# An expert layer in one block: gate and up products made while VectorE routes, eight of them multiplied on GpSimd

## The chip, the cores and the metric

The kernel runs on one NeuronCore of a Trainium2 chip. The metric is the device time of one execution in microseconds. TensorE (PE) multiplies matrices into eight PSUM banks of 128x512 f32; VectorE (DVE) and ScalarE (ACT) read and write PSUM and SBUF; GpSimd (POOL) works on SBUF only; SyncE (SP) issues transfers.

## The reference, cut to what matters

A decoder of four layers over 1024 tokens of 128 features. Every sublayer's output is added to x and normalised. The sublayer in question is the expert layer of the third layer, L2_ffn: a mixture of 8 experts of 176 hidden units, with the two best experts of each token.

```
probs = softmax(x @ router_w.T); topk_w, topk_idx = top_k(probs, 2)
topk_w = topk_w / (sum(topk_w) + 1e-20)
combine = sum(topk_w[..., None] * one_hot(topk_idx, E), axis=1)
for e in range(E):
    g = x @ w_gate[e].T;  u = x @ w_up[e].T
    ye = silu(g) * u @ w_down[e].T
    out = out + combine[:, e:e + 1] * ye
```

## The kernel before

x is kept in SBUF as 128 features by 1024 tokens. The 8 x 176 hidden units lie side by side as M = 11 groups of 128; with two halves of 512 tokens that makes 22 items (m, h), and every token goes through every expert, weighted with `combine`, which is zero for those not chosen. A stage is a row of blocks; all engines leave a block before any begins the next, and the semaphores are cleared between. L2_ffn has four blocks before its norm.

- Router, by the helper `stream` (L136): eight f32 matmuls of x against the router's 8 columns into one bank (recorded at L163), and VectorE copies the 64 logits to `probs` (L1901). SyncE starts the next stage's weights.
- Route (L1903 to L1953): VectorE makes the softmax (Exp on ScalarE, L1911), the eight largest (L1925) and their places (L1928), the shares of the first two, `combine` (L1941), and splits it into three bf16 parts in `parts` (L1944 to L1947). GpSimd clears `parts` (L1951), casts the 0/1 matrix `spread` to bf16 (L1952) and centres w_down by the helper `weight_centring` (L217, L221, L222). TensorE has nothing in this block.
- Turn (L1954): eight bf16 matmuls turn `parts`, and VectorE copies two banks to `partsT` (L1957).
- Experts (L1958 to L2008): `centre_tokens` (L230) starts the sums in banks 6 and 7. Then for item j three matmuls (L1975): gate, up, and spread against `partsT`, which gives the item's weight for each token. They go into banks 0 to 2 or 3 to 5 by j's parity. ScalarE takes the silu of gate (L1997), VectorE multiplies with up (L2007) and with spread (L2008) into `hidden`, and TensorE adds w_down's product to bank 6 or 7 (L1982). TensorE's order is up(0), up(1), down(0), up(2), down(1), ...; up(j) waits until item j-2 is multiplied, down(j) until item j is.

The norm that follows reads banks 6 and 7. Engines run their instructions in order.

Of the kernel before, what the change touches and what calls it, by code (L numbers as in the profile page):

```python
# [20 lines left out]
ACT = mybir.ActivationFunctionType  # L21
ALU = mybir.AluOpType
# [179 lines left out]
def weight_centring(K, stack, tag, groups, scratch=None):  # L202

    nc = K.nc
    if scratch is None:
        scratch = stack.enter_context(nc.sbuf_tensor(f"{tag}_weight_sums", [P, groups, P // 2], F32))
    sem = Sems(nc, stack, tag + "_centre")
    own, ready = sem("pool_own"), sem("weights_centred")  # L210

    def centre(pool, w):
        chain = Chain(pool, own)
        w, half = w.rearrange("p (g c) -> p g c", c=P), P // 2
        src = w
        while half >= 1:
            chain.link(nc.gpsimd.tensor_tensor(scratch[:, :, 0:half], src[:, :, 0:half], src[:, :, half:2 * half],  # L217
                                               ALU.add))
            src, half = scratch, half // 2
        mean = scratch[:, :, 0:1]  # L220
        chain.link(nc.gpsimd.tensor_scalar(mean, mean, 1 / P, None, ALU.mult))  # L221
        nc.gpsimd.tensor_tensor(w, w, mean.to_broadcast([P, groups, P]), ALU.subtract).then_inc(ready, 1)  # L222
    return centre, ready
# [757 lines left out]
def halves(ap):  # L981
    return [ap[:, h * HALF:(h + 1) * HALF] for h in range(2)]
# [896 lines left out]
def L2_ffn(K):  # L1879
# [7 lines left out]
    with ExitStack() as stack:  # L1887
        def sb(name, shape, dt=F32):
# [6 lines left out]
        parts, rest = sb("parts", [P, 2 * B, 3, 32], BF16), sb("rest", [P, 2 * B, E])  # L1895
        partsT, spread = sb("partsT", [96, T], BF16), sb("spread", [96, M * P], BF16)
        silu, hidden = sb("silu", [P, 2, HALF]), sb("hidden", [P, 2, HALF])
        centre_w_down, _ = weight_centring(K, stack, "L2_ffn", M)
        stream(K, "L2_ffn_router", [
            ("dve", P, [(c * E, E, [(x[:, c * P:(c + 1) * P], W("router"))]) for c in range(2 * B)],  # L1900
             lambda bank: nc.vector.tensor_copy(probs[:].rearrange("p c e -> p (c e)"), bank[:, 0:2 * B * E]))],  # L1901
            on_sync=K.fetch_next)
        with ExitStack() as inner:  # L1903
            sem = Sems(nc, inner, "L2_ffn_route")
            own, shifted, exp_done, cleared = sem("dve_own"), sem("shifted"), sem("exp_done"), sem("cleared")
            block = inner.enter_context(nc.Block())

            @block.scalar
            def _(act):
                act.wait_ge(shifted, 1)  # L1910
                nc.scalar.activation(probs[:], probs[:], ACT.Exp).then_inc(exp_done, 1)  # L1911

            @block.vector
            def _(dve):
                chain = Chain(dve, own)
                wide = lambda ap: ap.to_broadcast([P, 2 * B, E])
                chain.link(nc.vector.tensor_reduce(stat[:], probs[:], AX.X, ALU.max))
                nc.vector.tensor_tensor(probs[:], probs[:], wide(stat[:].unsqueeze(2)), ALU.subtract
                                        ).then_inc(shifted, 1)
                dve.wait_ge(exp_done, 1)  # L1920
                chain.link(nc.vector.tensor_reduce(stat[:], probs[:], AX.X, ALU.add))
                chain.link(nc.vector.reciprocal(stat[:], stat[:]))
# [21 lines left out]
                chain.link(nc.vector.tensor_copy(part[0], combine[:]))  # L1944
                chain.link(nc.vector.tensor_tensor(rest[:], combine[:], part[0], ALU.subtract))
                chain.link(nc.vector.tensor_copy(part[1], rest[:]))
                nc.vector.tensor_tensor(part[2], rest[:], part[1], ALU.subtract)  # L1947

            @block.gpsimd
            def _(pool):  # L1950
                nc.gpsimd.memset(parts[:], 0.0).then_inc(cleared, 1)  # L1951
                nc.gpsimd.tensor_copy(spread[:], W("spread"))  # L1952
                centre_w_down(pool, W("w_down"))  # L1953
        stream(K, "L2_ffn_turn", [  # L1954
            ("dve", 96, [(c * P, P, [(parts[:, 4 * c4 + c].rearrange("p r e -> p (r e)"), K.ident_bf)])
                         for c in range(4)],
             lambda bank, c4=c4: nc.vector.tensor_copy(halves(partsT)[c4], bank[0:96, :])) for c4 in range(2)])  # L1957
        with ExitStack() as inner:  # L1958
            sem = Sems(nc, inner, "L2_ffn_experts")
            up_done, silu_done, own, hidden_done, down_done = (sem(n) for n in (  # L1960
                "up_done", "silu_done", "dve_own", "hidden_done", "down_done"))
            block = inner.enter_context(nc.Block())

            items = [(m, h) for m in range(M) for h in range(2)]

            @block.tensor
            def _(pe):
                def up(j):
                    m, h = items[j]
                    if j >= 2:  # L1970

                        pe.wait_ge(hidden_done, j - 1)
                    for n, (w, rhs) in enumerate(((W("w_gate"), halves(x)[h]), (W("w_up"), halves(x)[h]),
                                                  (spread, halves(partsT)[h]))):
                        last = nc.tensor.matmul(K.bank[3 * (j % 2) + n][:], w[:, m * P:(m + 1) * P], rhs,  # L1975
                                                start=True, stop=True)
                    last.then_inc(up_done, 1)

                def down(j):
                    m, h = items[j]  # L1980
                    pe.wait_ge(hidden_done, j + 1)
                    nc.tensor.matmul(K.bank[6 + h][:], W("w_down")[:, m * P:(m + 1) * P], hidden[:, j % 2], start=False, stop=(m == M - 1),  # L1982
                                     skip_group_check=True).then_inc(down_done, 1)
                centre_tokens(K, K.bank[6:8])
                for j in range(len(items) + 1):
                    if j < len(items):
                        up(j)
                    if j >= 1:
                        down(j - 1)

            @block.scalar
            def _(act):
                for j in range(len(items)):
                    act.wait_ge(up_done, j + 1)
                    if j >= 2:
                        act.wait_ge(hidden_done, j - 1)
                    nc.scalar.activation(silu[:, j % 2], K.bank[3 * (j % 2)][:], ACT.Silu).then_inc(silu_done, 1)  # L1997

            @block.vector
            def _(dve):  # L2000
                chain = Chain(dve, own)
                for j in range(len(items)):
                    dve.wait_ge(silu_done, j + 1)
                    if j >= 2:
                        dve.wait_ge(down_done, j - 1)
                    hj = hidden[:, j % 2]
                    chain.link(nc.vector.tensor_tensor(hj, silu[:, j % 2], K.bank[3 * (j % 2) + 1][:], ALU.mult))  # L2007
                    nc.vector.tensor_tensor(hj, hj, K.bank[3 * (j % 2) + 2][:], ALU.mult).then_inc(hidden_done, 1)  # L2008
        norm_of_centred(K, "L2_ffn_norm", K.bank[6:8])


# [646 lines left out]
```

## Time and profile before

| | |
|---|---|
| time, median of 3 | 1590.61 us (1590.35 to 1593.66) |
| profiled execution, its own time | 1582.52 us |
| its span, first to last instruction | 1580.7 us |
| TensorE busy | 1209.8 us, 77% |
| VectorE / ScalarE / GpSimd busy | 984.1 / 881.5 / 543.8 us |
| granted TensorE clock, mean | 0.892 |

The profile is one execution. Each row has a start from the span's begin and a duration; matmuls overlap in their pipeline, so their durations sum to more than the time. The granted clock is 1.00 at 2.4 GHz and 0.50 at 1.2 GHz. L2_ffn lies between 951 and 1035 us.

### The profile page before, as it was taken

Reading aid. Unit: us, or ns where it says so; the run is one execution under the profiler, and the core shown is the slowest. Engines: PE = TensorE matmul, PEld = TensorE weight load, DVE = VectorE, ACT = ScalarE, POOL = GpSimd, SP = SyncE. Lnnn points to the kernel's source line nnn. Section 1 sums busy time; section 2 is a strip of 40 time slices with the busy share of each in tenths; the row PEclk is TensorE's granted clock in tenths of the full one; section 3 lists DMA queues with packets and bytes.
Section 4 is the critical chain, followed back from the end, with each engine's and each line's share of the span. In section 5 each row is a group of like instructions: output and inputs, shape, how many; then the busy total and the mean of one; then the engine's idle time right before and its main releaser. Section 6 shows DMA issues by size and latency. Waiting matters only on the chain. (4 is left out here: it accounts for less than half of the span.)

```text
span 1580.7 us, 21176 instructions
## 1 busy us (share of the span) xinstructions
PE 1209.8 (77%) x6990; PEld 607.2 (38%) x6990; DVE 984.1 (62%) x1994; ACT 881.5 (56%) x1817; POOL 543.8 (34%) x673
## 2 busy tenths in 40 slices
PE   8999647266666677987657995977968988979886
PEld 3675422022222233542213552433444434734562
DVE  3673455999999927632757735446546658727752
ACT  3674144599999926874124871234634745724643
POOL 1462014488888843200224212011101223503440
PEclk9999887599999987998877997987986999999998
DMA  3000000000000015101006200015114110000000
GB/s 149 2 2 1 22 9 0 0 0 0 1 0 0 0 73 141 22 34 40 0 3 196 50 2 18 0 33 124 16 56 125 37 56 1 2 1 1 1 2 13
DMA packets 44108, 48.75 MB, mean 31 GB/s; under 512 B 3808, under 2 KB 40800, under 8 KB 42848
## 3 DMA queue, kind: packets, MB, share of 16 engines
q1 hardware_dynamic: 40688, 45.83, 10.0%
q10 hardware_dynamic: 3312, 1.57, 0.3%
q8 instruction: 56, 0.92, 0.3%
q14 instruction: 52, 0.43, 0.1%
HBM read 34.28 MB, written 13.11 MB: 30 GB/s over the span
## 5 line engine op out<-in xcount | busy, mean ns | idle before, releaser
L1548 POOL TENSOR_TENSOR L_attn_z<-L_attn_state,L_attn_r 128x1024 f32<-128x1024 f32 x64 | 151.0, 2360 | 21.6 <-DVE L_attn_state L1534 14.7
L1534 DVE TENSOR_TENSOR_SCAN L_attn_state<-bank,L_attn_w 128x512 f32<-128x512 f32 x128 | 148.9, 1205 | 0.0
L1445 PE MATMUL bank<-L_attn_z,const 128*128 128x512 f32 x256 | 139.4, 673 | 0.2 <-POOL L_attn_z L1552 0.2
L950 DVE CUSTOM_DVE_ANT_0 L_xattn_core_logits<-bank,L_xattn_mask 128x256 f32<-128x256 f32 x256 | 98.6, 422 | 45.1 <-PE bank L722 32.6
L1429 PE MATMUL bank<-L_attn_rows,L_attn_select 128*128 128x512 bf16 x96 | 36.2, 435 | 79.5 <-ACT L_attn_C L1497 42.9
L1485 ACT ACTIVATE L_attn_r<-L_attn_after_dt,L_attn_half_guard,L_attn_A 128x512 f32<-128x512 f32 x128 | 96.5, 802 | 0.0
L1475 ACT ACTIVATE bank<-L_attn_dt,L_attn_A 128x510 f32<-128x510 f32 x128 | 86.5, 676 | 12.8 <-DVE L_attn_state L1534 12.8
L862 ACT ACTIVATE L_xattn_core_probs<-bank 128x512 f32<-128x512 f32 x132 | 71.6, 596 | 35.6 <-PE bank L765 24.5
L1552 POOL TENSOR_TENSOR L_attn_z<-L_attn_z,L_attn_C 128x1024 f32<-128x1024 f32 x32 | 75.8, 2368 | 23.4 <-ACT L_attn_C L1497 23.3
L1515 DVE TENSOR_TENSOR L_attn_w<-bank,L_attn_udt 128x1024 f32<-128x1024 f32 x64 | 78.2, 1221 | 5.3 <-PE bank L1429 1.6
L722 PE MATMUL bank<-L_xattn_core_rows 48*128 48x256 bf16 x384 | 61.3, 302 | 17.2 <-DVE L_xattn_core_top L950 11.9
L1445 PEld LDWEIGHTS bank<-L_attn_z,const 128*128 128x128 f32 x256 | 54.3, 212 | 49.2 <-issue 39.8
L543 POOL TENSOR_TENSOR L_attn_core_probs<-L_attn_core_probs,L_attn_core_rsum 128x256 f32<-128x256 f32 x64 | 51.6, 827 | 60.5 <-DVE L_attn_core_rsum L512 60.5
L543 POOL TENSOR_TENSOR L_ffn_core_probs<-L_ffn_core_probs,L_ffn_core_rsum 128x256 f32<-128x256 f32 x64 | 51.6, 829 | 45.9 <-DVE L_ffn_core_rsum L512 45.9
L2313 PE MATMUL bank<-L_ffn_shifted,weights 128*128 128x512 f32 x128 | 61.1, 622 | 8.0 <-PEq L2232 8.0
L217 POOL TENSOR_TENSOR L_attn_weight_sums<-weights 128x64 f32<-128x64 f32 (+1 forms) x3 | 1.1, 365 | 191.0 <-POOLq L306 110.8
L1491 ACT ACTIVATE L_attn_r<-L_attn_r 128x1024 f32<-128x1024 f32 x64 | 66.7, 1043 | 0.0
L163 PE MATMUL bank<-x,weights 128*128 128x512 f32 (+1 forms) x108 | 52.9, 639 | 12.8 <-PEq L306 5.8
L2399 POOL TENSOR_TENSOR L_ffn_part<-L_ffn_part 128x512 f32<-128x512 f32 x32 | 40.8, 1274 | 61.4 <-DVE L_ffn_part L2378 61.4
L920 POOL TENSOR_TENSOR shiftsT<-L_xattn_core_top,nothing 128x8 bf16<-128x8 f32 x48 | 12.1, 253 | 142.3 <-DVE L_xattn_core_top L950 95.6
L477 ACT ACTIVATE L_ffn_core_probs<-bank,L_ffn_core_negmax 128x128 f32<-128x128 f32 (+1 forms) x128 | 52.0, 428 | 9.6 <-DVE L_ffn_core_negmax L503 9.6
L750 PE MATMUL bank<-L_xattn_core_rows 48*128 48x256 bf16 x384 | 56.7, 283 | 0.4
(500 smaller groups left out, 3042.9 us busy)
## 6 DMA issues: line engine op xcount, KB each, us to landing
L_xattn_core_rows<-L_xattn_core_slots SPq DMA_DIRECT2D x48, 96.0 KB, 2.3
L_xattn_core_rows<-L_xattn_core_slots SPq DMA_DIRECT2D x12, 384.0 KB, 6.1
weights<-in_pack_L_ffn SPq DMA_DIRECT2D x2, 2118.5 KB, 8.1
L_xattn_core_slots<-L_xattn_core_k_parts SPq DMA_DIRECT2D x24, 128.0 KB, 2.1
weights<-in_pack_L_ffn SPq DMA_DIRECT2D x1, 2824.0 KB, 12.3
L_xattn_core_slots<-L_xattn_core_q_parts SPq DMA_DIRECT2D x9, 192.0 KB, 2.2
weights<-in_pack_L_xattn SPq DMA_DIRECT2D x1, 1539.5 KB, 6.3
weights<-in_pack_L_attn SPq DMA_DIRECT2D x2, 768.0 KB, 9.4
```

What stands on the lines that cost most here:

```text
L543: last = nc.gpsimd.tensor_tensor(part, part, rsum[:, i % NB, :, sc:sc + 1].to_broadcast([P, 2, keys[sc].stop]), ALU.mult)
L722: last = nc.tensor.matmul(scores_bank[side][:, c * S:(c + 1) * S], row(QUERIES, side, p, c), row(KEYS, side, p), start=True, stop=True)
L862: nc.scalar.activation(probs[n % 3][:, at], shifted_bank[at][:], ACT.Exp).then_inc(exp_done, 1)
L950: last = nc.vector.tensor_tensor_reduce(logits[:, c], scores_bank[side][:, c * S:(c + 1) * S], mask[:, 2 * b + c, :], 1.0, MASKED, ALU.add ...
L1445: last = nc.tensor.matmul(y_bank[2 * c + half][:], ident, z[:, g % NS, c], start=False, stop=False, skip_group_check=True)
L1475: nc.scalar.activation(two(a_bank[c][:])[:, :, lo:lo + S - 1], two(dt[d][:, c, tokens(half)])[:, :, lo:lo + S - 1], ACT.Exp, scale=A[d][:, ...
L1485: last = nc.scalar.activation(r[:, g % NS, c], after_dt[d][:, c, tokens(half)], ACT.Tanh, bias=half_guard[:], scale=A[d][:, 1, at:at + 1])
L1491: nc.scalar.activation(r[:, g % NS], r[:, g % NS], ACT.Copy, scale=0.5, bias=0.5).then_inc(r_done, 1)
L1515: nc.vector.tensor_tensor(w[:, g % 2], B_bank[:].unsqueeze(1).to_broadcast([P, DC, HALF]), udt[d][:, :, tokens(half)], ALU.mult).then_inc( ...
L1534: nc.vector.tensor_tensor_scan(state[:, g % NS, c, ::step], a_bank[c][:, ::step], w[:, g % 2, c, ::step], 0.0, ALU.mult, ALU.add).then_inc ...
L1548: nc.gpsimd.tensor_tensor(z[:, g % NS], state[:, g % NS], r[:, g % NS], ALU.mult).then_inc(z_done, 1)
L1552: nc.gpsimd.tensor_tensor(z[:, g % NS], z[:, g % NS], copied[:, g // 2 % 2].unsqueeze(1).to_broadcast([P, DC, HALF]), ALU.mult).then_inc(p ...
```

## The change

The four blocks become one. TensorE does the router into bank 2, the centring matmuls, then gate and up (without spread) of items 0 to 9. For items 0 to 7 (EARLY = 8) ScalarE empties both banks, silu of gate and a copy of up, into a new SBUF tile `ahead` (32 KB a partition), and GpSimd multiplies the two after it has centred w_down. Items 8 and 9 stay in the banks. up(j) waits for the copies of item j-2, as far as there are any. Then TensorE waits for `parts`, turns them through banks 2 and 5, waits for `spread`, `partsT` and the centred w_down, and goes through the items: up(j) from j = 10 on, spread as a step of its own, `weigh(j)`, which waits until item j-2 is multiplied, and down(j-1). VectorE multiplies an early item once (`ahead` by the spread bank) and the other 14 twice, as before. ScalarE waits for gate and up, no longer for spread.

```diff
-        centre_w_down, _ = weight_centring(K, stack, "L2_ffn", M)
-        stream(K, "L2_ffn_router", [
-            ("dve", P, [(c * E, E, [(x[:, c * P:(c + 1) * P], W("router"))]) for c in range(2 * B)],
-             lambda bank: nc.vector.tensor_copy(probs[:].rearrange("p c e -> p (c e)"), bank[:, 0:2 * B * E]))],
-            on_sync=K.fetch_next)
+        centre_w_down, w_down_ready = weight_centring(K, stack, "L2_ffn", M)
+        EARLY = 8
+        ahead = sb("ahead", [P, EARLY, 2, HALF])
...
+            spread_bank = K.bank[2:6:3]
...
+            @block.sync
+            def _(sp):
+                K.fetch_next(sp)
+
+            @block.tensor
+            def _(pe):
+                def up(j):
+                    m, h = items[j]
+                    if 2 <= j < EARLY + 2:
+                        pe.wait_ge(taken_ahead, 2 * min(EARLY, j - 1))
+                    elif j >= 2:
+                        pe.wait_ge(hidden_done, j - 1)
+                    for n, w in enumerate((W("w_gate"), W("w_up"))):
+                        last = nc.tensor.matmul(K.bank[3 * (j % 2) + n][:], w[:, m * P:(m + 1) * P], halves(x)[h],
+                                                start=True, stop=True)
+                    last.then_inc(up_done, 1)
+
+                def weigh(j):
+                    m, h = items[j]
+                    if j >= 2:
+                        pe.wait_ge(hidden_done, j - 1)
+                    nc.tensor.matmul(spread_bank[j % 2][:], spread[:, m * P:(m + 1) * P], halves(partsT)[h],
+                                     start=True, stop=True).then_inc(spread_done, 1)
...
+                for c in range(2 * B):
+                    last = nc.tensor.matmul(spread_bank[0][:, c * E:(c + 1) * E], x[:, c * P:(c + 1) * P], W("router"),
+                                            start=True, stop=True)
+                last.then_inc(router_done, 1)
+                centre_tokens(K, K.bank[6:8])
+                for j in range(EARLY + 2):
+                    up(j)
+                pe.wait_ge(parts_ready, 1)
+                for c4 in range(2):
+                    for c in range(4):
+                        last = nc.tensor.matmul(spread_bank[c4][0:96, c * P:(c + 1) * P],
+                                                parts[:, 4 * c4 + c].rearrange("p r e -> p (r e)"), K.ident_bf,
+                                                start=True, stop=True)
+                    last.then_inc(turned, 1)
+                pe.wait_ge(spread_ready, 1)
+                pe.wait_ge(partsT_ready, 2)
+                pe.wait_ge(w_down_ready, 1)
+                for j in range(len(items) + 1):
+                    if j < len(items):
+                        if j >= EARLY + 2:
+                            up(j)
+                        weigh(j)
+                    if j >= 1:
+                        down(j - 1)
 
             @block.scalar
             def _(act):
                 act.wait_ge(shifted, 1)
                 nc.scalar.activation(probs[:], probs[:], ACT.Exp).then_inc(exp_done, 1)
+                for j in range(EARLY):
+                    act.wait_ge(up_done, j + 1)
+                    nc.scalar.activation(ahead[:, j, 0], K.bank[3 * (j % 2)][:], ACT.Silu).then_inc(taken_ahead, 1)
+                    nc.scalar.activation(ahead[:, j, 1], K.bank[3 * (j % 2) + 1][:], ACT.Copy).then_inc(taken_ahead, 1)
+                for j in range(EARLY, len(items)):
+                    act.wait_ge(up_done, j + 1)
+                    if j >= EARLY + 2:
+                        act.wait_ge(hidden_done, j - 1)
+                    nc.scalar.activation(silu[:, j % 2], K.bank[3 * (j % 2)][:], ACT.Silu).then_inc(silu_done, 1)
...
+                nc.vector.tensor_tensor(part[2], rest[:], part[1], ALU.subtract).then_inc(parts_ready, 1)
+                for c4 in range(2):
+                    dve.wait_ge(turned, c4 + 1)
+                    nc.vector.tensor_copy(halves(partsT)[c4], spread_bank[c4][0:96, :]).then_inc(partsT_ready, 1)
+                for j in range(len(items)):
+                    hj = hidden[:, j % 2]
+                    if j >= 2:
+                        dve.wait_ge(down_done, j - 1)
+                    if j < EARLY:
+                        dve.wait_ge(product_ahead, j + 1)
+                        product = ahead[:, j, 0]
+                    else:
+                        dve.wait_ge(silu_done, j - EARLY + 1)
+                        chain.link(nc.vector.tensor_tensor(hj, silu[:, j % 2], K.bank[3 * (j % 2) + 1][:], ALU.mult))
+                        product = hj
+                    dve.wait_ge(spread_done, j + 1)
+                    nc.vector.tensor_tensor(hj, product, spread_bank[j % 2][:], ALU.mult).then_inc(hidden_done, 1)
 
             @block.gpsimd
             def _(pool):
                 nc.gpsimd.memset(parts[:], 0.0).then_inc(cleared, 1)
-                nc.gpsimd.tensor_copy(spread[:], W("spread"))
+                nc.gpsimd.tensor_copy(spread[:], W("spread")).then_inc(spread_ready, 1)
                 centre_w_down(pool, W("w_down"))
...
+                for j in range(EARLY):
+                    pool.wait_ge(taken_ahead, 2 * (j + 1))
+                    nc.gpsimd.tensor_tensor(ahead[:, j, 0], ahead[:, j, 0], ahead[:, j, 1], ALU.mult).then_inc(product_ahead, 1)
```

The blocks of the turn and of the experts as they were are removed; `down(j)` is as it was.

## Rows read from the trace of the kernel before

**Rows 1.** Table of stretches (us; busy us and instructions by engine; granted clock; DMA).

```profile
951.10:953.20 2.10, 1.92 (x16) 1.86 (x16) 0.04 (x1) 0.00 (x0) 0.00 (x0) 1.00 0.46 112
953.20:956.00 2.80, 0.00 (x0) 0.00 (x0) 2.05 (x6) 0.26 (x1) 2.17 (x3) 0.57 0.38 155
956.00:965.30 9.30, 0.00 (x0) 0.00 (x0) 8.63 (x39) 0.00 (x0) 6.97 (x9) 0.50 0.00 1
...
971.00:1032.20 61.20, 61.01 (x153) 26.51 (x151) 29.00 (x43) 13.14 (x22) 0.00 (x0) 1.00 0.00 0
...
1034.70:1036.80 2.10, 0.00 (x0) 0.00 (x0) 0.00 (x0) 1.87 (x3) 0.00 (x0) 0.69 0.00 0
```

**Rows 2.** Timeline, TensorE, the router (start, duration, engine, line, operation, idle).

```profile
951.20 1.92 PE L163 MATMUL bank<-weights,x 128*128 128x8 f32 x16 [2.85 <-PEq L239]
```

**Rows 3.** Timeline, VectorE and GpSimd during the route.

```profile
953.83 0.74 POOL L1951 MEMSET L_ffn_parts<- 128x768 bf16 x1 [27.49 <-PEq L1903]
953.97 0.23 DVE L1918 TENSOR_TENSOR L_ffn_probs<-L_ffn_probs,L_ffn_stat 128x64 f32<-128x64 f32 x1
...
954.52 1.35 POOL L1952 CAST L_ffn_spread<-weights 96x1408 bf16<-96x1408 f32 x1
...
955.01 2.57 DVE L1923 TENSOR_TENSOR L_ffn_probs<-L_ffn_probs,L_ffn_stat 128x64 f32<-128x64 f32 x1
955.84 1.66 POOL L217 TENSOR_TENSOR L_ffn_weight_sums<-weights 128x704 f32<-128x704 f32 x1
...
961.05 2.56 POOL L222 TENSOR_TENSOR weights<-weights,L_ffn_weight_sums 128x1408 f32<-128x1408 f32 x1
...
964.96 0.23 DVE L1947 TENSOR_TENSOR L_ffn_parts<-L_ffn_rest,L_ffn_parts 128x64 bf16<-128x64 f32 x1
```

**Rows 4.** Timeline, from the turn to the first item of the loop.

```profile
965.45 0.88 PEld L163 LDWEIGHTS bank<-ident_bf,L_ffn_parts 128*96 128x96 bf16 x8 [12.42 <-issue]
...
966.15 1.28 DVE L1957 CAST L_ffn_partsT<-bank 96x512 bf16<-96x512 f32 x2 [0.97 <-PE bank L163]
967.72 1.28 ACT L1997 ACT_TABLE_LOAD   x1 [13.24 <-PEq L146]
...
967.76 3.39 PE L230 MATMUL bank<-x,const 128*128 128x512 f32 x4 [1.22 <-PEq L146]
...
970.98 1.88 PE L1975 MATMUL bank<-x,weights 128*128 128x512 f32 x4
...
975.22 1.13 PE L1982 MATMUL bank<-L_ffn_hidden,weights 128*128 128x512 f32 x2 [0.20 <-DVE L_ffn_hidden L2008]
```

**Rows 5.** Timeline, the loop: the fourth item, then the last.

```profile
978.97 1.88 PE L1975 MATMUL bank<-x,weights 128*128 128x512 f32 x4
...
1028.62 0.60 ACT L1997 ACTIVATE L_ffn_silu<-bank 128x512 f32<-128x512 f32 x1 [2.20 <-PE bank L1975]
...
1029.25 0.69 DVE L2007 TENSOR_TENSOR L_ffn_hidden<-L_ffn_silu,bank 128x512 f32<-128x512 f32 x1 [1.39 <-ACT L_ffn_silu L1997]
1029.29 1.88 PE L1975 MATMUL bank<-x,weights 128*128 128x512 f32 x4
...
1033.51 1.12 PE L1982 MATMUL bank<-L_ffn_hidden,weights 128*128 128x512 f32 x2 [1.27 <-DVE L_ffn_hidden L2008]
```

**Rows 6.** Groups by line and shape, GpSimd and ScalarE (count, busy, mean ns, idle).

```profile
L2399 POOL TENSOR_TENSOR L_ffn_part<-L_ffn_part 128x512 f32<-128x512 f32 x32 | 40.8, 1274 | 61.4 <-DVE L_ffn_part L2378 61.4
...
L868 ACT ACTIVATE L_xattn_core_gathered<-bank 128x512 f32<-128x512 f32 x4 | 2.4, 591 | 1.2 <-PE bank L781 1.2
```

**Rows 7.** Timeline, GpSimd and VectorE in an earlier stage.

```profile
270.83 2.17 POOL L1309 TENSOR_TENSOR L_attn_rows<-L_attn_left,L_attn_middle 32x1024 bf16<-32x1024 f32 x1
...
271.04 3.04 DVE L1348 SCALAR_TENSOR_TENSOR L_attn_dt<-L_attn_dt,L_attn_spare 128x1024 f32<-128x1024 f32 x1
```

**Rows 8.** Timeline, ScalarE in an earlier stage.

```profile
225.90 0.19 ACT L1276 ACTIVATE L_attn_half_guard<-const 128x1 f32<-128x1 f32 x1
...
227.36 1.06 ACT L1283 ACTIVATE L_attn_u<-L_attn_conv 128x1024 f32<-128x1024 f32 x1
```

More of the change, by code:

```diff
@@ new lines, in L2_ffn, with down @@
+        EARLY = 8
+        ahead = sb("ahead", [P, EARLY, 2, HALF])
+        items = [(m, h) for m in range(M) for h in range(2)]
+        with ExitStack() as inner:
+            sem = Sems(nc, inner, "L2_ffn_experts")
+            router_done, own, shifted, exp_done, cleared = (sem(n) for n in ("router_done", "dve_own", "shifted", "exp_done",
+                                                                            "cleared"))
+            spread_ready, parts_ready, turned, partsT_ready = (sem(n) for n in ("spread_ready", "parts_ready", "turned",
+                                                                                "partsT_ready"))
+            up_done, silu_done, taken_ahead, product_ahead = (sem(n) for n in ("up_done", "silu_done", "taken_ahead",
+                                                                               "product_ahead"))
+            spread_done, hidden_done, down_done = (sem(n) for n in ("spread_done", "hidden_done", "down_done"))
+            spread_bank = K.bank[2:6:3]
+            block = inner.enter_context(nc.Block())
+            @block.sync
[19 more added lines that the diff above has]
+                                     start=True, stop=True).then_inc(spread_done, 1)
+                def down(j):
+                    m, h = items[j]
+                    pe.wait_ge(hidden_done, j + 1)
+                    nc.tensor.matmul(K.bank[6 + h][:], W("w_down")[:, m * P:(m + 1) * P], hidden[:, j % 2], start=False,
+                                     stop=(m == M - 1), skip_group_check=True).then_inc(down_done, 1)
+                for c in range(2 * B):
[22 more added lines that the diff above has]
+                        down(j - 1)
@@ L1916, in _ @@
                 wide = lambda ap: ap.to_broadcast([P, 2 * B, E])
+                dve.wait_ge(router_done, 1)
+                chain.link(nc.vector.tensor_copy(probs[:].rearrange("p c e -> p (c e)"), spread_bank[0][:, 0:2 * B * E]))
                 chain.link(nc.vector.tensor_reduce(stat[:], probs[:], AX.X, ALU.max))
-                nc.vector.tensor_tensor(probs[:], probs[:], wide(stat[:].unsqueeze(2)), ALU.subtract
-                                        ).then_inc(shifted, 1)
+                nc.vector.tensor_tensor(probs[:], probs[:], wide(stat[:].unsqueeze(2)), ALU.subtract).then_inc(shifted, 1)
                 dve.wait_ge(exp_done, 1)
@@ L1951, in _ @@
                 nc.gpsimd.memset(parts[:], 0.0).then_inc(cleared, 1)
-                nc.gpsimd.tensor_copy(spread[:], W("spread"))
+                nc.gpsimd.tensor_copy(spread[:], W("spread")).then_inc(spread_ready, 1)
                 centre_w_down(pool, W("w_down"))
[L1954 to L2008, printed above, removed]
```

3 lines of the change are left out of this document (removed).

## The prediction

> **What bounds the kernel now.** I read the page first: TensorE is the busiest engine, but none bounds the whole, so the stage decides. The change touches only the expert layer, and the table of stretches cuts that layer into parts [rows 1]. From 951.1 to 953.2 TensorE does 16 tiny router matmuls; from 953.2 to 965.3 it does nothing while VectorE is busy 10.7 of 12.1 us (2.05 + 8.63, routing) and GpSimd 9.1; then come 2.5 us of turning the parts and, from 967.7, the centring matmuls [rows 4]; and from 971.0 to 1032.2 TensorE is busy 61.0 of 61.2 us. So the layer is a route during which TensorE waits, then a loop that TensorE alone bounds.
>
> The timeline gives the durations. A 512-column f32 matmul is two records; gate, up and down of an item are six, and the bf16 spread one that streams half as long. The gate of the fourth item starts at 978.97, that of the last at 1029.29: 18 further items of 2.795 us [rows 5]. At the full clock a record is thus 2.795 / 6.5 = 0.43 us at most; I take 0.427, so gate 0.85, up 0.85, down 0.85 and spread 0.21, together 2.77. The first gate starts at 970.98 [rows 4] and the last down ends at 1034.63 [rows 5]. ScalarE (0.60 for a silu) and VectorE (two products of 0.69) are hidden under TensorE's 2.80 [rows 5].
>
> **What the change does to TensorE's early part.** The router stays as it is and ends at 953.12 [rows 2]. Behind it now stand, without waiting for the route, the centring (1.71 us at the full clock) and ten times gate and up (10 x 1.71 = 17.07): 18.8 us, so to 971.9. Two things could hold it. ScalarE must empty two banks an item: silu 0.60, and a copy of the same size 0.59 [rows 6], 1.2 us against 1.71 of matmuls, so it keeps up. And the clock: it is at 2.4 GHz (granted 1.00) to 953.2 and falls in the stretch to 956.0 (mean 0.57, so at 953.6) to 1.2 GHz [rows 1], after 5 us in which TensorE had only the tiny router matmuls [rows 2]. All of that is unchanged but its last 0.5 us, so I expect the same fall. In the kernel before it was back after 2.9 us of dense work (967.76 to about 970.6) [rows 1, 4]. Here dense work begins at 953.15, so I take 3.4 us at half clock, 1.7 us lost: ups done at 973.6. Bounds: 971.9 without the fall, 975.3 with twice as long a one.
>
> **GpSimd and VectorE.** One block in place of four: GpSimd starts with the stage, 951.2 in place of 953.83, and its memset, cast and centring last 9.8 us (953.83 to 963.61) [rows 3], to about 961.0. w_down is then ready long before it is needed. Then eight products of 128x512, both inputs in SBUF. The nearest row is 1.27 us each [rows 6]; 10.2 us, back to back until it has caught up with ScalarE, done at about 972.6 (item 7 is taken at 971.4, plus one product).
>
> VectorE is where this hurts. An operation on two SBUF tiles of 128x64 takes it 0.23 us (953.97), but 2.57 at 955.01, when GpSimd has a cast and then a large sum running; it ends at 957.58, just after the sum (957.50) [rows 3]. It was issued during the cast and did not get in between cast and sum, which follow without a gap. Where GpSimd's instructions are a few hundredths apart (a chain between them), VectorE got in after one: 3.04 us in all, ending 1.1 us after GpSimd's of 2.17 us [rows 7].
>
> In the changed kernel the first subtraction of the route (953.7) waits for the sum of 704 columns (to 954.9). Exp ends at 955.5, ScalarE's table load of 1.28 follows and is ready before the first up is (958.2). The route's small operations then go on to about 959.1, where the share product meets the 2.56 us subtraction (958.9 to 961.4) and, gapless behind it, the train of products. ScalarE hands over item k at 959.4 + 1.71k, GpSimd could start it at 961.4 + 1.27k; the first gap is therefore in front of item 5, at 967.7. From there VectorE gets two or three of its eight remaining SBUF products into each gap of 0.45 us, and the rest after 972.6: `parts` complete at about 974.0. Without the clock's fall the train has no gap to 971.6 and 2.45 us of route follow: 974.0 again. If VectorE gets in between any two products it is one step per product, about 973; if it is not held at all, 964. What this costs is small because of its cover: TensorE is not free before 973.6 either. With the cover gone (ups done at 971.9) it would be 2.1 us.
>
> The skill has rules that speak against this change. The page "SBUF — State Buffer" of the Trainium skill, section "Who interferes with whom": a VectorE instruction with two SBUF inputs and a GpSimd one that reads SBUF exclude each other, whichever starts first, for the whole instruction. The trace agrees (2.57 us for 0.23). The page "Perfetto Trace Analysis" of the Trainium skill, section "Optimizing Scalar/DVE Operations", warns that moving work between the two might therefore not help. By these rules the route is longer by the whole train and the first spread (below) comes at 976.2; with no hold it would come at 975.7, since TensorE is busy to 973.6 anyway.
>
> **Turn.** In the kernel before, 1.98 us pass from the first weight load of the turn (965.45) to the end of the second copy (967.43) [rows 4]; the block boundaries beside it (parts complete at 965.19, centring begins at 967.76) go [rows 3, 4]. 974.05 + 1.98 + 0.15 for the first spread's load: the first spread (w_0) streams at 976.2.
>
> **The new loop**, from w_0, with a spread of 0.21 streaming and readable after 0.42, a product of 0.69 (+0.03), and an estimated 0.17 from its end to the streaming of the next down (weight load of 975.21 included; the product had ended at 975.16) [rows 4, 5]. Items 0 to 7 need one product only. Down 0 waits for spread and product, w_0 + 1.28; spread 2 follows at 2.13, and then TensorE's own work, 0.21 + 0.85 = 1.07, sets the pace: spread 8 at 8.55. Items 8 and 9 have both VectorE products (1.44) and no ups to hide them: down 8 at 10.33 in place of 9.83, up 10 at 11.18. From there the old period, 2.795: up 21 at 11.18 + 11 x 2.795 = 41.93. The tail was 1034.63 - 1029.29 = 5.34 [rows 5]; ScalarE now waits for gate and up only and not for the spread, minus 0.21: 5.13. Sum 47.06, end at 1023.3 against 1034.63: **11.3 us less**. Check by TensorE's work: centring and 22 items are 1.7 + 22 x 2.77 = 62.7 us, so from 953.1 the end would be at 1015.8 without any pause, 18.8 less; off go 1.7 (clock), 2.6 (973.6 to 976.2) and 3.1 in the loop (47.06 against 12 x 2.77 + 10 x 1.07), which leaves 11.4.
>
> The profiled execution took 1582.52 us for its span of 1580.7; the median of the runs shown is 1590.61, 8 us more, so I subtract: 1590.6 - 11.3 = 1579.3.
>
> **Rivals.**
> *A second fall of the clock* (0.25). Between the last up (973.6) and down 0 (977.5) TensorE has only the turn and two spreads. In the kernel before, a pause of 1.3 us with 1.1 us of work and another pause was enough for a fall at about 1036 (mean 0.69 from 1034.7 to 1036.8) [rows 1, 5]. It would hit items 0 to 4, where TensorE is the bound: about 1.7 us, so 9.6 less, 1581.0.
> *No hold and no fall* (0.15): ups done at 971.9, parts earlier: w_0 = 971.9 + 2.1 = 974.0 and 13.5 less, 1577.1.
> *The products or the route cost more* (0.11): GpSimd products of 1.6 us and VectorE held to their end: parts at 961.4 + 12.8 + 2.5 = 976.7, w_0 = 978.9, 8.6 less, 1582.0; with the second fall 6.9 less.
> *The early matmuls are not worth their place* (0.02): a TensorE still at half clock through all ten ups loses not 1.7 but up to 18 us, most of the gain; the clock's recovery in 2.9 us of dense work speaks against it.
> *Slower: ScalarE's tables* (0.02). If Silu and Copy each had to load a table (1.28 us), an early item would take 3.77 us of ScalarE, item 7 would be taken at 958.2 + 30.2 = 988.4, up 9 done at 990.1, w_0 = 992.3: 4.8 us slower, 1595.4. It decides from 2.0 us of loads per item. Against it: Copy, Copy and Silu follow one another at 225.9 to 228.4 with no load between [rows 8]; the load itself is 1.28 [rows 4].
>
> **Numbers.** The forecast itself has 0.45; its own range is 1578 to 1580.5. The range to hold it 8 times in 10 goes from the case without hold and fall to the dear route with margin for how the clock's falls lie in the rest of the kernel: 1576.0 to 1584.0. A measurement of this kernel can tell about 0.2% (3.2 us) from nothing. Faster by more (the first four cases): 0.96; within: 0.02; slower: 0.02.
>
> **What would show it.** Right: TensorE busy from 953 to about 973 with one halved stretch at its start; VectorE's share and pick products several us long while GpSimd multiplies; first spread near 976; spreads 1.07 us apart up to the ninth; last down 11 us earlier. Wrong: parts complete at 965 (no hold) or later than 976; granted clock 0.5 beyond 958 or about 978; eight or more table loads on ScalarE; an item period beyond 2.8 in the second part.

## The result and the profile after

| | kernel before | changed kernel |
|---|---|---|
| median | 1590.48 us (1588.62 to 1593.66, 4 runs) | 1577.94 us (1575.62 to 1579.96, 4 runs) |
| ratio | | 0.9927, 95% interval 0.9904 to 0.9951 |
| profiled execution, span | 1580.7 us | 1574.3 us |

The medians differ by 12.5 us, the two spans by 6.4. To see what the change did and what not, I cut each span at the issue of the stage's weights by SyncE (the one at 951.16 and the next, 1043.01, before; 951.74 and 1032.08 after). The stage with its norm took 91.85 us before and 80.34 after, 11.5 less; the end of the last down came 83.47 and 73.35 us after the stage's start, 10.1 less. All the rest took 1488.8 and 1493.9, though it is the same program in both. In the nine further profiles that leave the rest unedited (below) it took 1490.6 to 1495.4; the profile of the kernel before is the shortest of all. There is only one profile of that kernel, so whether this is chance isn't shown. Comparing the two spans understates what the stage gained by 5.1 us.

The page of the changed kernel, its span and the engines' busy time:

```profile
span 1574.3 us, 21154 instructions
...
PE 1212.7 (77%) x6990; PEld 609.5 (39%) x6990; DVE 983.2 (62%) x1986; ACT 885.3 (56%) x1825; POOL 555.6 (35%) x681
```

The table of stretches, answering to [rows 1] (us; busy us of PE, PEld, DVE, ACT, POOL; granted clock; DMA):

```profile
953.50:957.00 3.50, 3.50 (x7) 1.58 (x8) 2.80 (x6) 0.93 (x2) 3.36 (x3) 0.56 0.39 156
957.00:958.30 1.30, 1.30 (x3) 0.49 (x3) 1.23 (x17) 0.61 (x1) 1.13 (x3) 0.87 0.00 0
958.30:974.30 16.00, 16.00 (x40) 7.00 (x39) 11.51 (x23) 9.28 (x17) 13.37 (x13) 1.00 0.01 2
974.30:977.20 2.90, 1.13 (x11) 0.51 (x9) 1.96 (x4) 0.60 (x1) 0.00 (x0) 1.00 0.00 0
...
978.00:981.30 3.30, 3.30 (x6) 1.27 (x5) 0.69 (x1) 0.00 (x0) 0.00 (x0) 0.51 0.00 0
...
1027.00:1031.00 4.00, 1.98 (x4) 0.68 (x4) 0.69 (x1) 3.21 (x6) 0.00 (x0) 1.00 0.00 0
```

TensorE is now busy all of 953.5 to 974.3, where it had been idle for 12 us. The clock is halved once at the beginning, as foreseen: means of 0.56 to 957.0 and 0.87 from there to 958.3 make 3.4 us at half clock. It is halved once more from about 978 to 981.3. In the norm behind the stage (1027 to 1031) it is 1.00, where it had fallen in the kernel before (mean 0.69 from 1034.7 to 1036.8) [rows 1].

The timeline from the router to the loop, answering to [rows 2 to 4]:

```profile
951.78 1.92 PE L1945 MATMUL bank<-weights,x 128*128 128x8 f32 x16 [2.85 <-PEq L239]
...
952.95 1.35 POOL L2039 CAST L_ffn_spread<-weights 96x1408 bf16<-96x1408 f32 x1
...
953.56 3.42 PE L230 MATMUL bank<-x,const 128*128 128x512 f32 x4
...
954.26 1.76 DVE L1990 TENSOR_TENSOR L_ffn_probs<-L_ffn_probs,L_ffn_stat 128x64 f32<-128x64 f32 x1
954.27 1.66 POOL L217 TENSOR_TENSOR L_ffn_weight_sums<-weights 128x704 f32<-128x704 f32 x1
...
956.77 17.61 PE L1927 MATMUL bank<-x,weights 128*128 128x512 f32 x40
...
959.44 2.58 POOL L222 TENSOR_TENSOR weights<-weights,L_ffn_weight_sums 128x1408 f32<-128x1408 f32 x1
...
959.87 2.18 DVE L2006 TENSOR_TENSOR L_ffn_share<-L_ffn_top,L_ffn_stat 128x16 f32<-128x16 f32 x1
...
961.98 6.29 POOL L2043 TENSOR_TENSOR L_ffn_ahead<-L_ffn_ahead 128x512 f32<-128x512 f32 x5
962.09 1.24 DVE L2010 TENSOR_TENSOR L_ffn_pick<-weights,L_ffn_placef 128x64 f32<-128x64 f32 x1
...
967.05 1.30 DVE L2012 TENSOR_TENSOR L_ffn_combine<-L_ffn_pick 128x64 f32<-128x64 f32 x1
...
968.88 1.16 DVE L2017 CAST L_ffn_parts<-L_ffn_rest 128x64 bf16<-128x64 f32 x1
...
970.07 0.22 DVE L2018 TENSOR_TENSOR L_ffn_parts<-L_ffn_rest,L_ffn_parts 128x64 bf16<-128x64 f32 x1
...
974.23 0.61 PE L1954 MATMUL bank<-ident_bf,L_ffn_parts 128*96 128x128 bf16 x8
...
974.65 1.28 DVE L2021 CAST L_ffn_partsT<-bank 96x512 bf16<-96x512 f32 x2 [4.36 <-PE bank L1954]
...
976.03 0.59 PE L1935 MATMUL bank<-L_ffn_partsT,L_ffn_spread 96*128 96x512 bf16 x2 [1.20 <-issue]
...
977.27 1.57 PE L1941 MATMUL bank<-L_ffn_hidden,weights 128*128 128x512 f32 x2 [0.64 <-DVE L_ffn_hidden L2034]
...
983.44 1.02 PE L1941 MATMUL bank<-L_ffn_hidden,weights 128*128 128x512 f32 x2
...
985.66 1.02 PE L1941 MATMUL bank<-L_ffn_hidden,weights 128*128 128x512 f32 x2
```

Read it by engine. TensorE: router to 953.70, centring from 953.56, ten gate-and-up pairs in one run from 956.77 to 974.38, then the turn at 974.23, and after it 1.20 us of nothing until 976.03: it waits for VectorE's two copies (974.65 to 975.93). VectorE: the first subtraction (954.26) is issued at the same moment as GpSimd's sum of 704 columns and takes 1.76 us; the share product (959.87) takes 2.18 us and ends at 962.05, right after GpSimd's subtraction; the first pick, which takes 0.23 us alone, takes 1.24 beside the products, and so on to `combine`. GpSimd ran its first five products without a gap (6.29 us from 961.98), and VectorE got in between every two of them. A cast of VectorE (968.88) is held as well. `parts` are complete at 970.29, 18.55 us after the stage's start, and wait there 3.9 us for TensorE.

The loop's end, answering to [rows 5]; the period is still 2.79 us, and the norm's matmuls take 1.98 us at full clock:

```profile
1017.10 1.88 PE L1927 MATMUL bank<-x,weights 128*128 128x512 f32 x4
...
1019.89 1.88 PE L1927 MATMUL bank<-x,weights 128*128 128x512 f32 x4
...
1023.97 1.12 PE L1941 MATMUL bank<-L_ffn_hidden,weights 128*128 128x512 f32 x2 [1.12 <-DVE L_ffn_hidden L2034]
...
1027.33 1.98 PE L265 MATMUL bank<-L_ffn_norm_square,const 128*128 128x512 f32 x4 [2.23 <-ACT L_ffn_norm_square L277]
```

### The profile page after: what moved, and what is told of

The parts are those of the page before. It is cut to its first block and busy times, and to the rows that moved or that the text cites. A ratio compares the mean times of both kernels' runs of the same rounds, so it can differ in the third digit from the quotient of the medians.

```text
span 1574.3 us, 21154 instructions
## 1 busy us (share of the span) xinstructions
PE 1212.7 (77%) x6990; PEld 609.5 (39%) x6990; DVE 983.2 (62%) x1986; ACT 885.3 (56%) x1825; POOL 555.6 (35%) x681
## 3 DMA queue, kind: packets, MB, share of 16 engines
q1 hardware_dynamic: 40688, 45.83, 10.1%
## 5 line engine op out<-in xcount | busy, mean ns | idle before, releaser
L722 PE MATMUL bank<-L_xattn_core_rows 48*128 48x256 bf16 x384 | 61.0, 303 | 18.0 <-DVE L_xattn_core_top L950 11.6
```

The source lines that it names most:

```text
L722: last = nc.tensor.matmul(scores_bank[side][:, c * S:(c + 1) * S], row(QUERIES, side, p, c), row(KEYS, side, p), start=True, stop=True)
```

## The experiments

Times are counted from the stage's start (the issue of its weights) in one profiled execution each; the ratio is that of timed runs against the kernel before on the same chip.

| run | parts complete | first spread | last down ends | stage with norm | ratio (95%) |
|---|---|---|---|---|---|
| kernel before | 14.03 | 21.54 | 83.47 | 91.85 | |
| changed | 18.55 | 24.29 | 73.35 | 80.34 | 0.9927 (0.9904 to 0.9951) |
| r9, changed again | 18.56 | 24.30 | 73.35 | 80.34 | 0.9934 (0.9912 to 0.9955) |
| r8, block only | 12.58 | 18.20 | 79.76 | 88.16 | 0.9963 (0.9942 to 0.9984) |
| r1, two ahead | 12.58 | 14.72 | 76.73 | 83.89 | 0.9946 (0.9923 to 0.9969) |
| r3, small products | 12.66 | 24.29 | 73.35 | 81.74 | 0.9946 (0.9926 to 0.9966) |
| r4, products on VectorE | 12.58 | 24.29 | 74.34 | 82.10 | 0.9940 (0.9914 to 0.9967) |
| r11, wide products | 27.23 | 29.37 | 79.78 | 88.17 | 0.9969 (0.9947 to 0.9991) |
| r2, turn before item 8 | 18.55 | 22.98 | 70.43 | 77.46 | 0.9905 (0.9880 to 0.9929) |
| r10, the same again | 18.55 | 22.99 | 70.44 | 77.73 | 0.9910 (0.9879 to 0.9942) |
| r7, four ahead, no GpSimd | 12.57 | 16.11 | 70.73 | 78.07 | 0.9903 (0.9868 to 0.9937) |
| r5, filler | 20.43 | 22.66 | 71.72 | 78.82 | 0.9908 (0.9878 to 0.9937) |
| r6, turn and filler | 18.55 | 22.98 | 70.42 | 77.41 | 0.9916 (0.9889 to 0.9943) |

Timed runs of one kernel scatter by 3 to 16 us, so the ratios separate only the largest steps. The column of the last down differed by 0.01 us at most between the two profiles of the changed kernel, and between r2 and r10, which are one kernel too; the verdicts rest on it.

**r9, the changed kernel again.**

> The changed kernel once more, unedited, for a second execution under the profiler and more timed runs beside the kernel before. My theory: within the stage nothing differs but where the clock's falls lie: last down at 71.6 to 73.6 us from the stage's start (73.35 with the second fall, 71.7 without), time 10 to 13 us under the kernel before. Rival (the first result was luck of the clock elsewhere): 6 us or less under it.

The same to 0.01 us, with the same second fall; 11.4 us under the kernel before by the medians (1577.77 against 1589.15). The first result was not luck.

**r8, one block, nothing early.** How much is the merging alone?

```diff
-        EARLY = 8
+        EARLY = 0
...
-                centre_tokens(K, K.bank[6:8])
-                for j in range(EARLY + 2):
-                    up(j)
                 pe.wait_ge(parts_ready, 1)
                 (turn)
+                centre_tokens(K, K.bank[6:8])
...
-                        if j >= EARLY + 2:
-                            up(j)
+                        up(j)
```

> One block as in the changed kernel, but centring and all ups behind the turn, nothing early (EARLY = 0). What do the block boundaries and GpSimd's earlier start bring by themselves? With two items ahead the last down ended at 76.73, before at 83.47. My theory: parts complete at 12.6 in place of 14.03, boundaries gone, so 1.5 to 2.3 us: last down at 81.2 to 82.0. Rival (boundaries are the larger part of the 6.7 us): 79 or less.

Last down 3.7 us earlier than before, about twice what I expected; the 79 or less of the rival was not reached (79.76). Timeline of TensorE:

```profile
963.58 1.09 PE L1951 MATMUL bank<-ident_bf,L_ffn_parts 128*96 128x128 bf16 x8 [10.67 <-DVE L_ffn_parts L2015]
964.46 3.13 PE L230 MATMUL bank<-x,const 128*128 128x512 f32 x4
967.42 1.88 PE L1927 MATMUL bank<-x,weights 128*128 128x512 f32 x4
```

What I had missed: without the boundary TensorE starts the centring at 13.5 us, directly behind the turn, while VectorE still copies; in the kernel before it had to wait for the copies and the block, 16.6 [rows 4]. That is 3.1 of the 3.7 us: 1.45 of it because the route ends earlier (14.03 to 12.58; GpSimd's work, which holds it, starts 2 us sooner), the rest the boundary and the copies. Where the last 0.6 us come from was not looked into.

**r1, two items ahead** (`EARLY = 0`).

> The changed kernel with EARLY = 0: one block, but only items 0 and 1 have their gate and up made before the route ends, nothing goes through `ahead`, GpSimd multiplies nothing. My theory (the gain is TensorE's work put under the route): only the centring and 2 x 1.7 us of ups lie under the route in place of 18.8 us. First spread about 15 us after the stage's start in place of 24.3, but 20 items of 2.8 us follow: the stage (issue of the next weights to issue of the ones after) 86 to 87.5 us, against 91.85 before and 80.34 changed, so about half the gain. Rival 1 (most of the gain is the block boundaries): stage within 1.5 us of the changed kernel, 80 to 82. Rival 2 (boundaries are worth nothing and the clock eats the two ups): 90 to 92.

```profile
954.91 3.60 PE L1927 MATMUL bank<-x,weights 128*128 128x512 f32 x8
962.23 1.09 PE L1954 MATMUL bank<-ident_bf,L_ffn_parts 128*96 128x128 bf16 x8 [3.72 <-DVE L_ffn_parts L2018]
964.32 1.01 PE L1935 MATMUL bank<-L_ffn_partsT,L_ffn_spread 96*128 96x512 bf16 x2 [1.00 <-issue]
```

Last down at 76.73, 6.7 us less than before. Of the changed kernel's 10.1 us, 3.7 come with the block, 3.0 with the centring and two ups under the route, and only 3.4 with the eight items of `ahead`. My theory holds in kind, but the stage was 83.9 and not 86 to 87.5, so it overrated the eight. The reason is in the rows: TensorE waits only 3.7 us for the route here (to 962.23), since the route without products ends at 12.6 us. Ups beyond that moment are no longer under the route. These shares also hold what the clock does: here it is halved for nearly all of 6.9 us around the turn, in the changed kernel for 3.4, so not all of the 3.4 us is work moved.

```profile
961.70:968.60 6.90, 4.94 (x14) 2.33 (x15) 4.27 (x8) 0.00 (x0) 0.00 (x0) 0.51 0.02 4
```

**r3, GpSimd multiplies 32 of 512 columns.** Left out are the other 480 columns of the early products. Is the hold on VectorE on the path?

```diff
-nc.gpsimd.tensor_tensor(ahead[:, j, 0], ahead[:, j, 0], ahead[:, j, 1], ALU.mult)
+nc.gpsimd.tensor_tensor(ahead[:, j, 0, 0:32], ahead[:, j, 0, 0:32], ahead[:, j, 1, 0:32], ALU.mult)
```

> The changed kernel, but GpSimd multiplies only 32 of the 512 columns of each early item (left out: the other 480 columns of silu(gate) * up), so it holds VectorE hardly at all. My theory (the hold is covered, TensorE's ups end later): `parts` complete 3 to 5 us earlier, first spread and stage unchanged within 0.3 us (80.1 to 80.6), time the same. Rival (the hold sets the first spread): stage 2 us or more shorter.

VectorE's timeline; the picks are 0.23 us again:

```profile
958.82 2.18 DVE L2006 TENSOR_TENSOR L_ffn_share<-L_ffn_top,L_ffn_stat 128x16 f32<-128x16 f32 x1
961.03 0.23 DVE L2010 TENSOR_TENSOR L_ffn_pick<-weights,L_ffn_placef 128x64 f32<-128x64 f32 x1
...
963.12 0.23 DVE L2018 TENSOR_TENSOR L_ffn_parts<-L_ffn_rest,L_ffn_parts 128x64 bf16<-128x64 f32 x1
973.60 1.28 DVE L2021 CAST L_ffn_partsT<-bank 96x512 bf16<-96x512 f32 x2 [10.26 <-PE bank L1954]
```

`parts` are complete 5.9 us earlier (3 to 5 expected), and the first spread and the last down stand still to the hundredth (24.29, 73.35). The hold costs nothing here, because TensorE is busy until 22.5. (The stage with its norm is 1.4 us longer, all of it behind the last down, where the clock is halved again.)

**r4, the eight products on VectorE, in the loop.** GpSimd's loop of products is removed.

```diff
-                        dve.wait_ge(product_ahead, j + 1)
-                        product = ahead[:, j, 0]
+                        dve.wait_ge(taken_ahead, 2 * (j + 1))
+                        chain.link(nc.vector.tensor_tensor(hj, ahead[:, j, 0], ahead[:, j, 1], ALU.mult))
+                        product = hj
```

> The changed kernel with the eight early products silu(gate) * up made by VectorE in the loop from `ahead`, GpSimd makes none. My theory: the route is not held, but the first spread stays at 24.3 us from the stage's start since TensorE is busy until then; items 0 to 7 then go at VectorE's pace of 1.45 us in place of about 1.1: stage 82 to 84 us. Rival (GpSimd's help is worth nothing, as what it takes off the loop it puts on the route): stage 80 to 80.8.

Last down 1.0 us later: GpSimd's help is worth 1 us, below what I expected. The stage, 82.10, is in my range only because the norm took 0.8 us more. Once the clock is back, TensorE's timeline shows 1.33 us a down among the early items, against 1.08 to 1.14 with GpSimd (983.44 and 985.66 above are two downs apart):

```profile
983.67 1.13 PE L1940 MATMUL bank<-L_ffn_hidden,weights 128*128 128x512 f32 x2
...
985.00 1.12 PE L1940 MATMUL bank<-L_ffn_hidden,weights 128*128 128x512 f32 x2
```

**r11, GpSimd's instructions twice as wide.** This takes the cover away.

```diff
+        products = sb("products", [P, EARLY, 2, HALF])
...
-                        product = ahead[:, j, 0]
+                        product = products[:, j, 0]
...
-nc.gpsimd.tensor_tensor(ahead[:, j, 0], ahead[:, j, 0], ahead[:, j, 1], ALU.mult)
+nc.gpsimd.tensor_tensor(products[:, j], ahead[:, j], ahead[:, j, 1:2].to_broadcast([P, 2, HALF]), ALU.mult)
```

> The changed kernel with each of GpSimd's eight instructions twice as wide (128x1024, the second half is not used), about 2.36 us in place of 1.27. This takes the cover away: GpSimd is at work from 10.2 to 29.1 us. My theory as the trace has changed it (VectorE's operation on SBUF tiles gets in after every one GpSimd instruction, one step for each): the picks and the combine are each 2.36 us apart, about 9 steps are left when the train begins, so `parts` complete near the train's end, 27 to 30 us in place of 18.55, first spread at 29.5 to 32 in place of 24.29, last down 78 to 81 in place of 73.35. Rival 1 (VectorE is kept out until the train has ended): none of the pick products ends before 29. Rival 2 (the hold costs nothing at any length): last down within 0.5 us of 73.35.

GpSimd, then VectorE, then TensorE:

```profile
964.25 16.68 POOL L2043 TENSOR_TENSOR L_ffn_products<-L_ffn_ahead 128x1024 f32<-128x1024 f32 x8
```

```profile
964.35 2.10 DVE L2010 TENSOR_TENSOR L_ffn_pick<-weights,L_ffn_placef 128x64 f32<-128x64 f32 x1
...
972.73 2.04 DVE L2012 TENSOR_TENSOR L_ffn_combine<-L_ffn_pick 128x64 f32<-128x64 f32 x1
974.81 2.02 DVE L2015 CAST L_ffn_parts<-L_ffn_combine 128x64 bf16<-128x64 f32 x1
...
978.97 2.01 DVE L2017 CAST L_ffn_parts<-L_ffn_rest 128x64 bf16<-128x64 f32 x1
981.01 0.23 DVE L2018 TENSOR_TENSOR L_ffn_parts<-L_ffn_rest,L_ffn_parts 128x64 bf16<-128x64 f32 x1
```

```profile
981.29 1.09 PE L1954 MATMUL bank<-ident_bf,L_ffn_parts 128*96 128x128 bf16 x8 [4.63 <-DVE L_ffn_parts L2018]
```

Eight instructions of 2.085 us (I had expected 2.36) follow without a gap, and VectorE's picks, `combine`, two casts and the first remainder each take 2.0 to 2.1: one VectorE instruction for each of GpSimd's. The last one, after the train, is 0.23 again. `parts` come at 27.23, TensorE waits 4.63 us for them, and now the hold is on the path: first spread 5.1 us later, last down at 79.78, 6.4 later. The other 1.3 us come behind the first spread: this profile has 10.2 us at half clock (mean 0.50 from 980.3 to 990.5) in place of 3.4. Rival 1 falls (`combine` ended at 974.77, the train at 980.93), and so does rival 2.

**r2, the turn before item 8's ups.** What is the pause worth in which TensorE waits for the copies?

```diff
                 for j in range(EARLY + 2):
+                    if j == 8:
+                        pe.wait_ge(parts_ready, 1)
+                        (turn)
                     up(j)
-                pe.wait_ge(parts_ready, 1)
-                (turn)
```

> The changed kernel with the turn of `parts` put before the gate and up of item 8 on TensorE, so that VectorE's two copies lie under the ups of items 8 and 9. In the changed kernel `parts` were complete at 970.3 and the last up ended at 974.2, then TensorE paused some 1.5 us for the copies and the clock was halved from 977.9 to 981.3. My theory (that pause costs itself and brings the fall): first spread 1.2 us earlier, no stretch at 0.50 behind it, stage 77 to 78.5 us in place of 80.34. Rival (the fall comes anyway, from the light spreads and waits at the loop's start): stage 79 to 79.5.

```profile
955.49 14.38 PE L1927 MATMUL bank<-x,weights 128*128 128x512 f32 x32
969.71 0.61 PE L1954 MATMUL bank<-ident_bf,L_ffn_parts 128*96 128x128 bf16 x8
970.16 3.65 PE L1927 MATMUL bank<-x,weights 128*128 128x512 f32 x8
973.64 0.60 PE L1935 MATMUL bank<-L_ffn_partsT,L_ffn_spread 96*128 96x512 bf16 x2
974.88 1.13 PE L1941 MATMUL bank<-L_ffn_hidden,weights 128*128 128x512 f32 x2 [0.64 <-DVE L_ffn_hidden L2035]
```

The copies lie under the ups of items 8 and 9, the first spread comes 1.3 us earlier, no fall follows, and the last down comes 2.9 us earlier, at 70.43. No other edit brings the last down clearly earlier (r6, which contains this one, is at 70.42); by timed runs it stands at 0.9905 and, repeated, 0.9910. The edit takes away the wait and moves the turn at once, so which of the two spares the fall isn't shown.

> The version with the turn before item 8's ups once more, on the same chip as the changed kernel. In the profiles its last down came 2.9 us earlier. My theory: last down at 70.4 to 70.8 us, and its time 2 to 4 us under the changed kernel's, which the scatter of single runs may hide. Rival (its gain was only the absence of a fall by luck): last down at 72 or later in this profile.

In this repeat the last down is at 70.44, without the fall. Beside the changed kernel on the same chip (r9) its median is 2.8 us lower, 1574.95 against 1577.77; their intervals overlap, so that it is faster is shown by the profiles and not by the timed runs.

**r7, four items ahead, turn before item 5, no product on GpSimd** (r4's and r2's edits with `EARLY = 4` and `j == 5`).

> EARLY = 4 in place of 8, the turn before item 5's ups, and VectorE makes the four products in the loop; GpSimd multiplies nothing. Without GpSimd's products the parts were complete at 12.58 us, and the ups of items 0 to 4 end at about 13.8: TensorE has work at every moment until the copies are made under item 5. My theory (only TensorE's pauses count, not how many items are made early nor GpSimd's help): first spread at 15.7 to 16.3, last down at 70.2 to 71.6 us, as with eight on GpSimd and the turn early (70.43). Rival (eight items and GpSimd's products are worth their own 2 us or more): 72.5 or later.

Last down at 70.73: half the items ahead and no GpSimd give what r2 gives to 0.3 us, and 2.6 less than the changed kernel. What counts is that TensorE is never out of work until `partsT` is there; whether four or eight items are made early made no difference beyond that. Fewer than four were tried only with none through `ahead` (r1), where TensorE does run out of work.

**r5 and r6, matmuls that keep TensorE busy before the stage.** Three 128x512 matmuls at the end of the norm before, read by nobody.

```diff
+            for _ in range(filler):
+                nc.tensor.matmul(K.bank[7][:], K.w("average"), square[:, 1], start=True, stop=True)
```

> The changed kernel with three further 128x512 f32 matmuls (read by nobody, into bank 7) at the end of TensorE's part of the norm before the stage, where it otherwise waits 2.85 us. Question: is the half clock from 954.0 to 957.4 due to that idle time, and what is it worth? My theory: no halved stretch at the stage's start, TensorE's ups end 1.7 us earlier, and the first spread and the last down, which hang on them, come 1.5 to 1.8 us earlier (22.6 and 71.7 us from the stage's start in place of 24.29 and 73.35), if the second fall stays. Rival (the fall is hidden, since the route is held to 18.6 us and the copies come after it): less than 0.5 us.

The clock stays at 1.00 through the norm's end and the first of the stage:

```profile
952.20:955.30 3.10, 2.81 (x7) 0.97 (x6) 1.50 (x2) 1.94 (x4) 0.00 (x0) 1.00 0.00 0
...
957.20:960.70 3.50, 3.50 (x10) 1.59 (x10) 2.94 (x7) 1.10 (x2) 3.34 (x4) 1.00 0.31 130
```

First spread and last down come 1.6 us earlier: that is what the halved stretch at the start costs, and I had counted 1.7. `parts` are later (20.43), since TensorE hands over the ups sooner and all eight products now follow each other without a gap. It looks as if the fall had been due to the idle time before, but the next run doesn't bear that out.

> Both: the turn before item 8's ups, and the three further matmuls in the norm before. With the turn early the last down ended at 70.43 us. My theory: the gains add while TensorE is never out of work; but without the fall up 7 ends at 17.3 and the held parts come only at 18.6, so TensorE waits 1.3 us for them: last down 69.0 to 70.1, not the 68.7 of a plain sum. Rival (they add in full): 68.7 or less.

```profile
949.60:952.60 3.00, 2.75 (x7) 0.95 (x5) 1.50 (x2) 1.88 (x4) 0.00 (x0) 1.00 0.00 0
...
954.40:957.90 3.50, 3.50 (x7) 1.50 (x7) 2.84 (x6) 0.96 (x2) 3.34 (x4) 0.60 0.39 154
```

Here the stretch from 954.4 has a mean of 0.60: the clock fell in spite of the same filler, after 1.8 us of router matmuls, and everything is as in r2. The last down, 70.42, lies outside both my range and the rival's, and whether the two gains add was not tested. With the same filler the fall was absent in one profile and there in another, so filler is no safe cure, and that the idle time alone brings the fall isn't shown.

## Why the prediction was right, step by step

Forecast 11.3 us less, 1579.3; measured 12.5 less by the medians (ratio times 1590.5: 11.6, interval 7.8 to 15.3). 1577.94 lies within the wide range and just below the forecast's own, 1578 to 1580.5. Inside the profile the last down was to come 11.3 us earlier and came 10.1 earlier; the norm gave another 1.4. That the sum, 11.5, is so near the forecast is luck: a fall that I had not put into the sum and a gain in the norm that I had not seen nearly cancel.

- *TensorE's work goes under the route.* Right: busy 953.5 to 974.3. The ups ended at 22.6 us from the start, forecast 973.6 - 951.2 = 22.4. The first fall came, and r5, which has none, shows its price, 1.6 us. Its length of 3.4 us was a choice, not read from a row (the row gave 2.9 us from the start of dense work to full clock); 3.4 was measured. The rival that TensorE would stay at half clock through all ten ups is refuted by the same rows: 1.00 from 958.3.
- *VectorE kept out until the first gap.* Wrong in mechanism. I took one case [rows 3], an operation that did not get in between a cast and a sum, for the rule. In the changed kernel and in r11 it got in after every single GpSimd product, gap or none. The step from a cast to a sum that I had generalised from is another matter, and stays unexplained (last section). `parts` came at 18.55, forecast 22.8; my bound "one step per product" said about 21.8, still late, because GpSimd's train had gaps from 968.3 on and the route's last steps fell into them.
- *The hold is covered.* Right, r3: 5.9 us of hold, no effect on the first spread.
- *Turn and first spread* at 25.0, measured 24.29. The turn began when the ups were done, 22.5, and not with late `parts` at 22.9; and it was shorter at full clock (1.70 us from its first matmul, 974.23, to the last copy's end, against 1.95 in the kernel before, at half clock).
- *Loop* of 47.06 us from the first spread; measured 73.35 - 24.29 = 49.06. Right in its parts (downs 1.08 to 1.14 apart, period 2.79; r2, without the fall, took 70.43 - 22.98 = 47.45) but the second fall came. I had given it 0.25, as a rival, and had named a halved clock about 978 among the signs of being wrong; that sign came true. The fall was there in all six profiles with this order of the turn (changed, r9, r3, r4, r5, r11), and r2, r10, r6 and r7, which have no pause, have none. It deserved to be the forecast: the row that showed such a fall was on my own list. With it I would have said 9.6 for the last down; 10.1 was measured.
- *What I did not count:* the norm behind the stage. Its four matmul records took 3.78 us (at 1036.87) in the trace of before, at a clock of 0.50, and 1.98 at a clock of 1.00 after; 1.4 us in all. It is not sure to stay: from the last down to the next stage took 8.4 us before, 7.0 in both profiles of the changed kernel, but again 8.4 in r3, r8 and r11.
- *The other rivals.* No hold and no fall: refuted. Products dearer: 1.26 to 1.27 us each, as the row said. Tables: one load (956.33), none between Silu and Copy.

The count of TensorE's work (18.8 us at most, minus pauses) was sound, but it hid how the gain divides, by the last down and with each version's own halved stretches: 3.7 us are the merged block (mostly that the centring no longer waits for the copies, a term that was missing from my text), 3.0 the first two items, 3.4 the eight through `ahead`, of which 1.0 is GpSimd's.

## What to carry to other kernels

When one engine bounds a loop and waits before it, count how long it waits and move just that much of its work there; r7 did with four items and one engine less what the change did with eight. Then look for the next place where it waits: a step that others must finish (the turn) belongs before the last pieces of its own work, not behind them. And compare the stage's length between two marks in the trace, not the spans of two executions.

## What the runs showed of the hardware that was not expected

VectorE and GpSimd take turns on SBUF operands instruction by instruction, even when GpSimd's follow without a gap: eight VectorE instructions in a row took 2.0 to 2.1 us each beside GpSimd's of 2.085 (r11), and the four picks and `combine` 1.2 to 1.3 beside its 1.26 (changed). SBUF-to-SBUF casts of VectorE are held like products of two SBUF tiles (2.02 us for 0.20). The page "SBUF — State Buffer" of the Trainium skill, section "Who interferes with whom", lists casts among what can contend, and the trace agrees; who gets the port next, when both want it, it does not say, and that was the point here. GpSimd did not pay: its five products took 6.29 us, 1.26 each. One place does not fit: the operation at 955.01 in the kernel before, issued during a cast of GpSimd, did not get in before the sum behind it [rows 3]. The changed kernel repeats this closely: the subtraction of 954.26 was issued in the last 0.04 us of the same cast (952.95 to 954.30) and came through only after the sum, at 956.02. Why stays open.

A short pause brought the slow clock every time: in five profiles (changed, r9, r3, r4, r5) the small turn, 1.20 us of waiting, two spreads and 0.64 to 0.68 us of waiting were followed by 3.4 us at 1.2 GHz. In r11, with 4.63 us of waiting before the turn, it was 10.2 us. There was none where the turn lay among the ups (r2, r6, r7, r10). So the 1.3 us that r2 takes off the first spread became 2.9 at the last down.
